# One loop per token tile in place of three in the projections, and the queues of wproj loads and output stores exchanged

## What is computed

```python
x = x + attn(layernorm(x))
x = x + ffn(layernorm(x))

# attn, 16 heads of 64, window 128
g = x @ Wg.T + bg;  v = x @ Wv.T + bv
corr = (g_i . g_j) / (|g_i| |g_j| + 1e-8) * m          # m: j <= i and j >= i - 128
corr = (corr + 1) / 2
denom = mean_j(corr) + 0.5
fitness = 1 / (denom * sum_i(1 / denom))
out = softmax(corr * fitness where m) @ v;  return out @ Wo.T + bo

# ffn, 1024 -> 4096 -> 1024
y = square(relu(x @ W_fc.T)) @ W_proj.T
for 5 steps: mem = 0.9 * mem + y - (mem > 1); spike = (mem > 1)
return sum(spikes) / 5
```

## Time and profile before

| | us |
|---|---|
| median of 2 runs | 1720.63 (1714.88 to 1726.39) |
| the profiled execution | 1697.39 |
| its span, slowest core (core 0) | 1696.4 |
| spans of the eight cores | 1674.7 to 1696.4 |
| granted TensorE clock, mean | 0.773 to 0.779 |

### The profile page before, as it was taken

One profiled execution on the slowest core, in us unless ns is written; L12 is line 12 of the kernel. 1 busy time (PEld: TensorE's weight loads), 2 busy tenths in 40 slices (PEclk: granted clock), 3 DMA queues, 4 the chain that ended last, 5 costly groups with the idle time before them and its releaser, 6 DMA issues.

```text
span 1696.4 us, 16590 instructions; the slowest of 8 cores (1674.7 to 1696.4 us)
## 1 busy us (share of the span) xinstructions
PE 1021.6 (60%) x4632; PEld 431.5 (25%) x4632; DVE 681.1 (40%) x1639; ACT 673.0 (40%) x1467; POOL 104.6 (6%) x168
## 2 busy tenths in 40 slices
PE   0024555692555555555555787988498868878800
PEld 0022222241122222222222233333143323333300
DVE  1301222200555555555553103069504960296098
ACT  1354323330466666666665564045303531252000
POOL 1011221111000000000000010001000100010000
PEclk9998778796555555555556899999799989999955
DMA  9987665444000000000002344445444544454410
GB/s 182 223 179 139 92 94 105 101 112 112 12 1 1 1 1 1 1 1 1 1 1 74 113 125 149 135 139 161 143 122 122 160 153 136 133 161 149 137 43 31
DMA packets 78910, 158.72 MB, mean 94 GB/s; under 512 B 38627, under 2 KB 38884, under 8 KB 78820
## 3 DMA queue, kind: packets, MB, share of 16 engines
q0 software_dynamic: 56912, 81.80, 21.5%
q1 hardware_dynamic: 21908, 75.85, 14.3%
HBM read 147.15 MB, written 33.55 MB: 107 GB/s over the span
## 4 chain that ended last, share of the span: by engine, by line
DMA 30%; PE 26%; DVE 18%; issue 11%; ACT 8%; another core or an unknown queue 4%; POOL 1%; DVEq 1%; ACTq 0%; SPq 0%; POOLq 0%
PE psY L830 8%; DMA wpb<-wprojC 6%; DMA wstg<-wfcT 6%; PE psY L797 5%; DMA wstg<-wprojT 5%; DMA wfcb<-wfcC 5%; ACT PT L586 4%; PE psPV L600 4%; DMA wfcC<-wstg 3%; DMA wprojC<-wstg 3%; DVE memb L874 3%; DVE t1b L871 3%; PE psPT L577 3%; PE psD L477 2%
## 5 line engine op out<-in xcount | busy, mean ns | idle before, releaser
L797 PE MATMUL psY<-x2nT,wfcb 128*128 128x512 bf16 x1024 | 234.6, 385 | 47.8 <-DMA wfcb<-wfcC 46.7
L830 PE MATMUL psY<-wpb,h_sb 128*128 128x512 bf16 x1024 | 233.5, 384 | 19.4 <-DMA wpb<-wprojC 18.4
L600 PE MATMUL psPV<-PT,v_sb 128*64 128x128 bf16 x512 | 103.9, 307 | 110.8 <-ACT PT L586 110.8
L483 DVE SCALAR_TENSOR_TENSOR C<-psD,maskA_sb 128x256 f32<-128x256 f32 x240 | 101.1, 422 | 153.0 <-PE psD L477 150.0
L526 ACT ACTIVATE ebf<-C,fit 128x256 f32<-128x256 f32 x256 | 151.4, 591 | 2.3 <-DVE em L565 0.6
L577 PE MATMUL psPT<-ident_sb,em 128*128 128x128 bf16 x512 | 97.9, 294 | 86.2 <-DVE em L565 84.6
L797 PEld LDWEIGHTS psY<-x2nT,wfcb 128*128 128x128 bf16 x1024 | 98.0, 99 | 183.7 <-issue 78.3
L830 PEld LDWEIGHTS psY<-wpb,h_sb 128*128 128x128 bf16 x1024 | 97.8, 99 | 154.0 <-issue 47.9
L477 PE MATMUL psD<-g_sb 64*128 64x256 bf16 x256 | 99.3, 390 | 39.0 <-DMA wprojC<-wstg 35.2
L806 ACT ACTIVATE frb<-psY 128x512 f32<-128x512 f32 x128 | 76.6, 599 | 110.5 <-PE psY L797 110.4
L565 DVE SCALAR_TENSOR_TENSOR em<-ebf,rqb,maskA_sb 128x256 bf16<-128x256 f32 x240 | 113.0, 474 | 0.5 <-issue 0.5
(11 more groups left out here) (99 smaller groups left out, 1192.1 us busy)
## 6 DMA issues: line engine op xcount, KB each, us to landing
wfcb<-wfcC POOLq DMA_DIRECT2D x64, 512.0 KB, 4.2
wpb<-wprojC SPq DMA_DIRECT2D x64, 512.0 KB, 3.6
xa<-xin SPq DMA_DIRECT2D x32, 512.0 KB, 5.3
wstg<-wfcT POOLq DMA_DIRECT2D x32, 256.0 KB, 6.0
xpair<-xin SPq DMA_DIRECT2D x8, 1024.0 KB, 12.0
wfcC<-wstg POOLq DMA_DIRECT2D x16, 512.0 KB, 3.2
wstg<-wprojT POOLq DMA_DIRECT2D x16, 512.0 KB, 5.3
wprojC<-wstg POOLq DMA_DIRECT2D x16, 512.0 KB, 3.0
```

Of the source, the lines that this page charges most:

```text
L483: msk=(mask0_sb if qt == 0 else maskA_sb): h.scalar_tensor_tensor(C_sb[hb][:, 256 * qt:256 * qt + 256], psD[qb][:], 1.0, msk[:], ALU.mult, ...
L600: mpv = b.op("T", lambda h, h_i=h_i, hp=hp, qt=qt, q4=q4, pb=pb, half=half: h.matmul(psPV[pb][hp:hp + 64, 128 * (q4 % 2):128 * (q4 % 2) + ...
L797: mmt = b.op("T", lambda h, f=f, fp=fp, k=k, gi=gi: h.matmul(psY[f % 2][:], wfcb[fp % 2][:, 1024 * (f % 2) + 128 * k:1024 * (f % 2) + 128 ...
L830: last = b.op("T", lambda h, f=f, f2=f2, tti=tti, nh=nh, pj=pj: h.matmul(psY[pj][:], h_sb[:, 512 * f + 128 * tti:512 * f + 128 * tti + 128 ...
```

## The change

Three things. Loops 1, 2 and 3 become one: for each tile, normalise and transpose, then its G projection, then its V projection; the bodies are the same, and `tt` is `t`. In `emit_proj_scan` the loads of W_proj go from queue Y to queue G. The `out` stores go from G to Y, and those of the group before are emitted ahead of the W_proj loads of a proj, not behind its matmuls; the last four go to Y in their old place.

```diff
     tok_stats = b.op("V", ...)
+    psG_free = [None, None]
+    gtk_free = [None, None]
+    ...
+    tok_v = None
     for t in range(NT):
         ...
         tok_x1T = evs[-1]
-
-    psG_free = [None, None]
-    ...
-    g_toks = []
-    tok_g = None
-    for tt in range(NT):
+        tt = t
         ev2 = []
...
         g_toks.append(evs[-1])
         tok_g = evs[-1]
-
-    psV_free = [None, None]
-    tok_v = None
-    for tt in range(NT):
         for nh in range(2):
             vi = (tt * 2 + nh) % 2
...
     def emit_proj_scan(gi):
         nonlocal scan_free, h_free
+        while pend_outs:
+            tt0, ob0, tout0 = pend_outs.pop(0)
+            tst = b.dma("Y", f"out{tt0}", out[128 * tt0:128 * (tt0 + 1), :],
+                        ob0[:], waits=[tout0])
+            y_free[tt0 % 4] = tst
...
                 tok_wp[f2 % 2] = b.dma(
-                    "Y", f"wps{f2 % 2}", wpb[f2 % 2][:],
+                    "G", f"wps{f2 % 2}", wpb[f2 % 2][:],
                     wprojC[:, 2048 * f2:2048 * (f2 + 1)],
                     waits=[wpb_free[f2 % 2], tok_wcache])
...
         h_free = ("T", b.cnt["T"])
-        while pend_outs:
-            tt0, ob0, tout0 = pend_outs.pop(0)
-            tst = b.dma("G", f"out{tt0}", out[128 * tt0:128 * (tt0 + 1), :],
-                        ob0[:], waits=[tout0])
-            y_free[tt0 % 4] = tst
...
     emit_proj_scan(3)
     while pend_outs:
         tt0, ob0, tout0 = pend_outs.pop(0)
-        tst = b.dma("G", f"out{tt0}", out[128 * tt0:128 * (tt0 + 1), :],
+        tst = b.dma("Y", f"out{tt0}", out[128 * tt0:128 * (tt0 + 1), :],
                     ob0[:], waits=[tout0])
```

More of the change, by code:

```diff
@@ L275, in build_core @@
         waits=[tk6, tk4])
+    psG_free = [None, None]
+    gtk_free = [None, None]
+    gsq_free = [None, None]
+    rqx_free = [None, None]
+    ghat_free = [None, None]
+    psV_free = [None, None]
+    g_toks = []
+    tok_g = None
+    tok_v = None
     for t in range(NT):
```

## The result

| | before | changed |
|---|---|---|
| median of all runs, us | 1695.45 (18 runs, 1683.11 to 1726.39) | 1713.77 (19 runs, 1702.14 to 1735.89) |
| ratio, changed to before | | 1.0114, 95% interval 1.0082 to 1.0146 |
| span of core 0, profiled | 1696.4 | 1706.8 |

The changed kernel is slower by 1.1%, clear of its interval and within 2%. The forecast ratio was 1.0118.

The account below looks back on a forecast made before the run. Attention was taken to wait for the weight cache, and proj to be paced by TensorE with short weight waits. Terms −2 + 16 + 4 + 3 − 1 = +20 us, ratio 1.0118 on 1720.6, gave 1741 us, range 1709 to 1770.

Parts of the forecast that it names:

- sum of +20: Whole kernel: −2 + 16 + 4 + 3 − 1 = +20 us on the profiled execution, ratio 1.0118.
- Part 2: Proj stretches: wproj loads moved from SP to POOL lengthen each turn of both buffers; +16 us, from +8 to +21.
- Part 3: Transfers newly queued together: +4 at the start of proj(1) and proj(2), +3 on POOL, 0 for the x load.
- Part 1: Before attention: fused loop ends at 417 us, 10 before the weight cache, so it stays covered; −2, from −10 to +10.
- the fused loop ends last: Rival, before attention: every tile takes 22 us, attention starts at 437, in all +32, 1753 us; chance 0.12.
- upper bound: Proj stretches: POOL adds 0.64 us to every one of eight turns in four stretches, +21 us.
- lower bound: Proj stretches: POOL's price hides in SP's already late loads, 64.6 us a stretch, 258 in all, +8 us.
- The 0 for tile 9: X load behind the scan: lands sooner, but waits again for TensorE's matmuls of that tile, so 0 us.
- Part 4: End of the kernel: last output store from SP is issued faster and lands 0.6 us sooner; −1 us, two either way.
- POOL-bound proj stretches: Rival, proj: POOL's loads become the bound, stretches above 70 us, four +50, in all +54, 1775 us; chance 0.17.
- Hidden loads: Rival, proj: what makes loads late is not their queue, so moving them doesn't show; −3, 1718 us; chance 0.08.
- Warm attention: Rival, attention: TensorE enters without idling and runs at 2.4 GHz, −79 there, in all −59, 1661 us; chance 0.06.

Follow-up runs that it names:

- e1: Fused loop alone, both queues as in the kernel before; ratio to before 1.0042 (1.0003 to 1.0081), +7 us.
- d6: d5 with the fused loop added; ratio to before 0.9852 (0.9799 to 0.9905), median 1670.86 us.
- d5: d4 with each x2r load also waiting for the last x2w issued; ratio to before 0.9751 (0.9703 to 0.9799), median 1653.60 us.
- e5: e1 with x loads in the fused loop only for the first two tiles; one profile, cache's last store issued at 393.8 us against 414.7.
- e2: Kernel before with only the wproj loads moved to POOL; ratio to before 1.0139 (1.0062 to 1.0216).
- d4: d1 with all weight loads (wfcb, wpb) on SP, output stores and x2r loads on POOL; ratio to before 0.9805 (0.9755 to 0.9856).
- e4: Changed kernel with the three loops of before, so both queue changes without the fusion; ratio to before 1.0121 (1.0053 to 1.0189).
- d1: Kernel before, but attention no longer waits for the weight cache, whose buffer lives through attention; ratio to before 0.9894 (0.9858 to 0.9929), −18 us.
- e3: Kernel before with only the output stores moved to SP, ahead of the wproj loads there; ratio to before 1.0113 (1.0079 to 1.0148), +19 us.

## Why the forecast came out as it did

**The absolute time.** The forecast put 1741 us and the measured median is 1713.8. The ratio forecast, 1.0118, lies in the measured interval; the step that failed is the last one of the sum, which multiplied it onto the median of two runs, 1720.6. With 18 runs that median is 1695.5, and 1695.5 x 1.0118 is 1715.5; against it the forecast of 1741 stands for +45 us, and +18 was measured. The text had noted that the profiled execution, 1697.4, was 1.4% below the two runs, and followed the runs. It also put 0.74 on a change of less than 2%, as one that can't be told from none, and that reading failed too: 1.1% was told apart, with an interval of 0.3% on either side. The sum of +20 was right by luck, since two terms were off by 10 us each in opposite ways, and Part 2 was too small by about what Part 3 was too large.

**Part 1, the fused loop.** Its length is right (20.7 us a tile, end at 415.0; forecast 20.85 and 417), and so is what covers it: e1 is nearly free, d6 against d5 costs 17. The term was mis-sized, −2 for a measured +7.7 in the profile of the change and 4 to 8 in e1. Two steps of it failed. One took the 1.25 us that a crowded x load costs the cache for what a spread one costs at most; but the second half of the cache, which no x load had met before, now takes 7 us longer (under e5), and the last store is some 4 us later on the mean of all profiles. The other took the cache's end on core 0, 426.8, for the cover on every core. Core 0 was the slowest core and its cache the latest: cores 1 to 3 started attention at 412.9, 411.8 and 409.2. The fused loop ends at 412 to 414 on these cores and attention follows 2 us behind at the soonest, so there was no slack of 10 us there but none, and whatever the cache does, attention starts later than before. In the change's own profile the cache ended last on all four cores, its last store 7.7 us later than before, so that +7.7 is the cache's; how it parts into spreading and scatter that one profile can't say. The rival "the fused loop ends last", at 0.12, had the right mechanism under too narrow a condition: it asked for slow tiles, and with ordinary ones three cores of e1 already waited for the loop.

**Part 2, wproj on POOL.** Right in mechanism, shown by e2 one way and by d4 the other. The size was +16 of a range of 8 to 21; e2 measured +23.1, above the upper bound. The step that failed is that bound: 0.64 us a turn is the difference between two quiet turns, and a turn grew by 0.72 in the median. Most turns in e2 are not quiet ones. Its timeline of TensorE in proj(1), core 0:

```profile
1229.28 3.61 PE L830 MATMUL psY<-wpb,h_sb 128*128 128x512 bf16 x16 [1.04 <-DMA wpb<-wprojC]
1234.32 7.07 PE L830 MATMUL psY<-wpb,h_sb 128*128 128x512 bf16 x32 [1.42 <-DMA wpb<-wprojC]
```

SP's late loads and POOL's price add, where the lower bound had one hide in the other. That bound was also taken from too short a sum: 249.9 us holds 60.5 for proj(3), whose matmuls span 62.3, and from first to last matmul the four are 252.9 on core 0, which makes it +5 and not +8. The estimate that the Trainium skill (DMA: Bandwidth & Descriptors, Specifications) led to, 13 us, is further off. The landing times differ by a little less than its first-byte difference of about 0.4 us: 3.94 us for wproj on POOL (e2) and 3.64 on SP, in the medians. The larger part of the price is POOL's start behind the matmul that frees the buffer, 0.54 us against SP's 0.08 (the rows under e2).

**Part 3, what is queued with what.** The stores and x2r loads in front of proj(1) and proj(2) were put at +4, and no cost of theirs shows (e4 against e2). The three loads in one POOL queue at the end of a proj were put at +3; what is left for it and for the stores in front of proj(3) is +2.6 and the excess of proj(3). The 0 for tile 9 was wrong by −9.8. The sentence that failed said that TensorE's matmuls of that tile need about as long as the load. The matmuls that stand in the timeline there are tile 10's; those of tiles 8 and 9 were done before the scan ended, as in e2, core 0, where the scan ends at 1193:

```profile
1185.10 1.89 PE L714 MATMUL psY<-woT_sb,x1T 128*128 128x512 bf16 x8
...
1187.44 1.90 PE L714 MATMUL psY<-woT_sb,x1T 128*128 128x512 bf16 x8
```

```profile
1198.92 1.29 DVE L722 TENSOR_TENSOR x2t<-psY,xa 128x512 f32<-128x512 f32 x2 [1.87 <-DMA xa<-xin]
```

So tile 9's residual waits for its x load alone, and what the load gains is gained. SP in the changed kernel, core 0:

```profile
1197.79 0.32 SPq L72 DMA_DIRECT2D x2d<-x2t  x1
1198.15 0.43 SPq L72 DMA_DIRECT2D xa<-xin  x1
1203.78 0.32 SPq L72 DMA_DIRECT2D x2d<-x2t  x1
```

From tile 8's x2w to tile 9's it takes 6.0 us; before, it took 11.2 on core 0, with the load of the earlier trace rows in between, and 10.5 to 12.7 on cores 1 to 3. The x load itself lands after 4.0 to 4.6 us on the eight cores, and took 8.2 to 10.8 before.

**Part 4** had −1 and measured −0.3: the sooner issue is there, the sooner landing is not.

**The rivals.** POOL-bound proj stretches above 70 us: proj(3) only, 70.6 on the mean, and with +22.4 for the four in place of +50 its price didn't come. The scan does add more under POOL's loads than under SP's: fc(3), by the row from proj(2) to proj(3), is 6.5 us longer than fc(0) in d1 and 3.1 in d4; what makes that difference of 3.4 no run here shows. Hidden loads: excluded by e2. Warm attention: excluded, at a granted 0.50 in all of 490 us, though TensorE idled only 8.7 us before it (core 0), and at 0.50 in d1 too, where it idled 1.5.

**The range** of 1709 to 1770 held the time. Its lower end did that, by way of the scatter of medians; with the two runs' median taken out, the same parts would have given 1692 to 1742 around 1715.

## What to carry to other kernels

Slack under a transfer must be read on every core, since a wait that is 35 us long on the slowest core was 18 to 27 on others, and an edit that fills it takes away slack that some cores never had. Before hiding work under such a transfer, ask who waits for it: here nothing in attention read the cache, and letting it go brought 18 us (d1) where filling the gap cost 7 (e1). Before a DMA is moved to another queue, list what stands behind it when its own wait is long (e3), and what else is released by the same instruction, since a load on the critical path pays for three strangers that leave with it (d4).

## What the runs showed of the hardware

- The same 512 KB loads make a double-buffered stretch of sixteen 5 us longer from POOL than from SP, in both directions (e2: proj 63.6 to 68.4, 5.8 on the mean of the four; d4: fc(0) 67.8 to 62.5). Their median landing differs by only 0.2 to 0.3 us (wpb 3.64 and 3.94, wfcb 3.80 and 4.04); the issue behind the releasing matmul, 0.08 us and 0.54, is the larger part.
- One 512 KB load on SP beside three that leave POOL within 2 us lands after 8.2 to 10.8 us on the eight cores (9.4 on core 0), beside one store after 5.0 to 6.1 (d5), and with none beside it after 4.0 to 4.6 (the change).
- Attention's 490 us did not react to what TensorE did before it, 35, 9 or 1.5 us of idling, nor to the cache's transfers beside it: from the start of attention to fc(0) it is 526.1 us on the mean of the cores in both before and d1.
- The fastest kernel tried, d5, is 2.5% faster than before and 3.5% faster than the change (1653.6 us against 1713.8).
